# Twelve-layer decoder: the attention stacks written within SBUF instead of by way of DRAM

## The reference

```python
Q = jnp.einsum('bsd,ed->bse', x_q, Wq) + bq
K = jnp.einsum('bsd,ed->bse', x_k, Wk) + bk
Qh, Kh = Q.reshape(b, sq, H, DH), K.reshape(b, -1, H, DH)          # H = 16, DH = 8
scores = jnp.einsum('bqhd,bkhd->bhqk', Qh, Kh) / math.sqrt(DH)
scores = scores + jnp.where(mask[:, None, None, :], 0.0, -1000000000.0)
out = jnp.einsum('bhqk,bkhd->bqhd', jax.nn.softmax(scores), Vh)
```

## Time and profile before

| | us |
|---|---|
| median of 3 runs | 4762.9 (4759.52 to 4770.97) |
| the profiled execution | 4766.7 |
| its span, first to last instruction | 4764.2 |
| TensorE busy | 3496.6 (73%) |
| VectorE busy | 2955.6 (62%) |
| ScalarE, GpSimd busy | 1970.0 (41%), 1234.1 (26%) |
| TensorE's granted clock, mean | 0.833 |

### The profile page before, as it was taken

One profiled execution on the slowest core, in us unless ns is written; L12 is line 12 of the kernel. 1 busy time (PEld: TensorE's weight loads), 2 busy tenths in 40 slices (PEclk: granted clock), 3 DMA queues, 4 the chain that ended last, 5 costly groups with the idle time before them and its releaser, 6 DMA issues. The chain is left out here.

```text
span 4764.2 us, 69288 instructions
## 1 busy us (share of the span) xinstructions
PE 3496.6 (73%) x25546; PEld 2337.3 (49%) x25546; DVE 2955.6 (62%) x6919; ACT 1970.0 (41%) x3470; POOL 1234.1 (26%) x1568
## 2 busy tenths in 40 slices
PE   5868867666878878665886887856589698685674
PEld 3645635334665555433575654533357465352353
DVE  4436874884554785577545488477654548738646
ACT  2423545343343444543344355434235335443333
POOL 0001451550000243253000045145100005516410
PEclk7989978777988988777898998877789799786776
DMA  7110121313121021032122112122211200211321
GB/s 237 46 47 14 39 81 42 103 55 106 66 79 62 28 76 58 29 130 73 47 100 69 39 36 81 45 88 84 104 56 52 98 10 28 80 54 45 117 101 49
DMA packets 174905, 328.00 MB, mean 69 GB/s; under 512 B 13260, under 2 KB 114988, under 8 KB 173740
## 3 DMA queue, kind: packets, MB, share of 16 engines
q1 hardware_dynamic: 174572, 323.59, 20.1%
HBM read 231.87 MB, written 91.67 MB: 68 GB/s over the span
## 5 line engine op out<-in xcount | busy, mean ns | idle before, releaser
L1881 PE MATMUL bank<-sb_big,sb_weights_const 128*128 128x512 f32 x512 | 376.6, 826 | 333.9 <-DVE sb_big L2119 333.2
L1434 POOL TENSOR_TENSOR sb_rs<-sb_ve,sb_weights_const 128x4 f32<-128x4 f32 x112 | 113.4, 1012 | 1757.6 <-DVE sb_ve L1420 1757.3
L1997 POOL TENSOR_TENSOR sb_big<-sb_big 128x512 f32<-128x512 f32 x384 | 496.4, 1307 | 244.9 <-DVE sb_big L2097 244.3
L1958 ACT ACTIVATE bank<-sb_big,sb_Aneg 128x512 f32<-128x512 f32 x512 | 351.7, 689 | 497.4 <-DVE sb_big L2114 392.3
L1252 DVE TENSOR_REDUCE sb_small<-bank 128x4 f32<-128x308 f32 (+1 forms) x512 | 265.9, 523 | 344.5 <-PE bank L967 340.9
L2114 DVE TENSOR_TENSOR_SCAN sb_big<-bank,sb_big 128x512 f32<-128x512 f32 x384 | 464.6, 1210 | 6.6 <-ACT bank L1958 6.3
L988 PE MATMUL bank<-sb_big 128*77 128x128 bf16 (+1 forms) x2560 | 358.1, 234 | 83.7 <-DMA sb_big<-key_parts 30.3
L988 PEld LDWEIGHTS bank<-sb_big 128*77 128x77 bf16 (+1 forms) x2560 | 274.2, 117 | 140.2 <-issue 89.8
L967 PE MATMUL bank<-sb_big 128*128 128x77 bf16 (+1 forms) x2048 | 187.4, 227 | 179.5 <-DMA sb_big<-query_parts 114.2
L1677 PEld LDWEIGHTS bank<-sb_weights_L1f,sb_big 128*128 128x128 f32 x2048 | 257.3, 191 | 109.0 <-issue 104.9
L1137 ACT ACTIVATE sb_big<-bank 77x512 f32<-77x512 f32 (+1 forms) x352 | 207.9, 593 | 228.3 <-PE bank L1009 152.4
(11 more groups left out here) (344 smaller groups left out, 8111.7 us busy)
## 6 DMA issues: line engine op xcount, KB each, us to landing
sb_big<-query_parts SPq DMA_DIRECT2D x160, 512.0 KB, 6.5
sb_big<-state_rows SPq DMA_DIRECT2D x128, 512.0 KB, 3.8
query_parts<-sb_big SPq DMA_DIRECT2D x120, 384.0 KB, 3.3
sb_big<-key_parts SPq DMA_DIRECT2D x64, 512.0 KB, 8.9
sb_big<-context_key_parts SPq DMA_DIRECT2D x64, 308.0 KB, 3.6
key_parts<-sb_big SPq DMA_DIRECT2D x48, 384.0 KB, 4.1
context_key_parts<-sb_big SPq DMA_DIRECT2D x48, 231.0 KB, 4.1
sb_big<-masked_key_parts SPq DMA_DIRECT2D x32, 308.0 KB, 3.5
```

The source lines that it names most:

```text
L1881: pe.matmul(m.bank[s][2][:, :], m.const["ident"], M.h(s, 2 * (n % 2)), start=n == 0, stop=n == NS - 1)\
L1958: act.activation(M.dA(s, half), M.dl(s, half), ACT.Exp, scale=m.Aneg[:, NS * half + n:NS * half + n + 1])\
L1997: pool.tensor_tensor(M.h(s, 2 * (n % 2) + half), M.b_rows(s, n // 2)[:, n % 2, :], M.du(s, half), ALU.mult)\
```

## The change

The stacks are no longer written to DRAM and read back. `heads_stack_sp` takes the place of both helpers: once the low part is made it issues nine transfers from SBUF to SBUF, one for each pair (i, j), each moving one part (128 partitions x 1 KB, for a context's keys 616 bytes) to eight partitions of the stack (16 heads x 1 KB each), and then one that reads the 56 rows below from DRAM, where they still lie since the start. For L1x it first waits for the masked keys' row in DRAM. TensorE waits once, before the first unit, for all ten transfers of both stacks; its waits at the later groups of heads are gone. `heads_sp` no longer has a due time of its own for the reads.

```diff
-    wq="query parts are in DRAM", wk="key parts are in DRAM", wm="the masked keys' row is in DRAM",
-    rq0="query stacks, heads 0 to 3", rq1="query stacks, heads 4 to 7",
...
+    wm="the masked keys' row is in DRAM",
+    rq="a copy of a query part is in its stack", rk="a copy of a key part is in its stack",
...
     def stacks(u):
-        if u % 4 == 0:
-            pe.wait_ge(*g.landed("rq%d" % (u // 4), A.key))
-            pe.wait_ge(*g.landed("rk%d" % (u // 4), A.key))
+        if u == 0:
+            pe.wait_ge(*g.landed("rq", (A.key, "below")))
+            pe.wait_ge(*g.landed("rk", (A.key, "below")))
...
-def heads_write_sp(sp, g, m, A, name):
-    s = g.s
+def heads_stack_sp(sp, g, m, A, name):
+    s = g.s
+    stack = A.q(s) if name == "q" else A.k(s)
     sp.wait_ge(*g.at("proj_d", (A.key, name, "low")))
-    dst = A.dram(s, name)[0:USED].rearrange("(i j d) h n -> (d h) i j n", i=3, j=3)
-    for copy in range(3):
-        sp.dma_start(dst[:, :, copy, :] if name == "q" else dst[:, copy, :, :], A.parts(s, name))\
-          .then_inc(*g.landing("w" + name, (A.key, copy)))
-def heads_read_sp(sp, g, m, A, name):
-    s = g.s
-    for each in name:
-        sp.wait_ge(*g.landed("w" + each, (A.key, 2)))
-    for group in range(4):
-        h = slice(4 * group, 4 * group + 4)
-        for each in name:
-            stack = A.q(s) if each == "q" else A.k(s)
-            sp.dma_start(stack[0:A.rows, h, :], A.dram(s, each)[0:A.rows, h, :])\
-              .then_inc(*g.landing(f"r{each}{group}", A.key))
+    if name == "k" and A.masked:
+        sp.wait_ge(*g.landed("wm", A.key))
+    for i in range(3):
+        for j in range(3):
+            sp.dma_start(stack[8 * (3 * i + j):8 * (3 * i + j) + DH, :, :],
+                         A.parts(s, name)[:, i if name == "q" else j, :])\
+              .then_inc(*g.landing("r" + name, (A.key, i, j)))
+    sp.dma_start(stack[USED:A.rows, :, :], A.dram(s, name)[USED:A.rows, :, :])\
+      .then_inc(*g.landing("r" + name, (A.key, "below")))
...
         yield A.time(A.split_at(i) + 1.1)
-        heads_write_sp(sp, g, m, A, name)
-    yield A.time(A.split_at(len(names) - 1) + 3.5)
-    heads_read_sp(sp, g, m, A, "".join(names))
+        heads_stack_sp(sp, g, m, A, name)
```

More of the change, by code:

```diff
@@ L227 @@
     rb1="an odd pair of rows of B is on all partitions",
-    wq="query parts are in DRAM", wk="key parts are in DRAM", wm="the masked keys' row is in DRAM",
-    rq0="query stacks, heads 0 to 3", rq1="query stacks, heads 4 to 7",
-    rq2="query stacks, heads 8 to 11", rq3="query stacks, heads 12 to 15",
-    rk0="key stacks, heads 0 to 3", rk1="key stacks, heads 4 to 7",
-    rk2="key stacks, heads 8 to 11", rk3="key stacks, heads 12 to 15",
+    wm="the masked keys' row is in DRAM",
+    rq="a copy of a query part is in its stack", rk="a copy of a key part is in its stack",
 )
@@ L1381, in heads_early_sp @@
         yield 0.01
[L1382 to L1386, removed]
+        heads_stack_sp(sp, g, m, A, "k")
 def heads_sp(sp, g, m, A):
```

## The result

The changed kernel takes 5522.1 us (median of 4 runs, 5513.5 to 5531.7) where the kernel before took 4761.2 us on the same chip: a ratio of 1.160, 95% interval 1.1575 to 1.1622. It is slower, as forecast, but by 761 us instead of 451, and 182 us above the upper end of the range.

The account below looks back on a forecast made before the run. Bound: TensorE idle for the stacks, 4% of the span, latency of a way with two legs. Added waits of 539 us x 0.8 = 431, plus 20 for the clock, +451 on 4766.7: 5214 us, range 4760 to 5340.

Parts of the forecast that it names:

- The landing rate, 1.7 us a transfer: Each SBUF-to-SBUF transfer of 128 KB into eight partitions of a stack takes 1.7 us, nine 15.3 us; chance 0.48.
- The upper bound of 5.1 us: Landing in eight partitions at no more than 25.9 GB/s: 5.1 us for 128 KB; as a rival 6480 us, chance 0.04.
- The rows below, 2.5 us,: The tenth transfer of a stack, 0.9 MB from DRAM at 14/16 of 414 GB/s, adds 2.5 us after the nine.
- Issuing: SyncE issues a stack's ten transfers at 0.43 to 0.49 us each, 4.6 us, hidden behind their landing.
- full rate: Rival: a transfer into a stack lands in 0.39 us, SyncE's issuing at 0.43 is the limit; 4712 us, chance 0.13.
- The pass-through of 0.8: Of the 539 us of added wait for stacks, 0.8 reaches the end of the kernel: 431 us.
- single: Context attentions, only the queries' stack waited for: 19.2 us against 8.9, 21 times, 188 us after spare time.
- pair: L0a and L3a, both stacks on the way: 37.0 us against 15.0, 12 times, 259 us after spare time.
- triple: Stream 0's L0a stacks and stream 1's L2x queries together: 54.8 us against 27.6, 3 times, 82 us.
- The clock,: After a wait TensorE goes on at half clock, some 2.5 us lost, newly at about eight waits: 20 us.
- SyncE's queue: The other stream's state rows in L2a queue behind a stack's transfers and come later; counted in the range.
- Only engines are halved: Rival: transfers into a stack use eight engines without crowding, 0.79 us each; 4847 us, chance 0.30.

Follow-up runs that it names:

- e1: Changed kernel with each copy placed on every ninth row of the stack instead of eight neighbouring rows: 4962 us, ratio 1.0428.
- e5: Kernel before, with TensorE waiting ahead of the first unit for all four groups' reads of both stacks: 4920 us, ratio 1.0333.
- e2: Changed kernel with copies on every second row, the ninth copy still on eight neighbouring rows: 5179 us, ratio 1.0903.
- e9: Changed kernel with every ninth row, queries' high and mid copies issued as made, most rows below read during the layer norm: 4787 us, ratio 1.0062.

## Why the prediction was wrong, point by point

- **What bounds the kernel** was right: the added wait reached the end, and the other engines' work did not change.
- **The landing rate, 1.7 us a transfer, is the term that failed most.** Measured 2.0 to 2.2 us (65 to 59 GB/s): the nine were there after some 21 us, where 1.4 + 9 x 1.7 = 16.7 was taken, and the wait grew by 765 us instead of 539. I had worked out 2.1 us from the slow fill and then taken 1.7, on the ground that engines which finish early go on to the next block of partitions. The copies landed one behind the other at an even pace instead. The fill at 376 GB/s, which I weighed against a limit by ports, *reads* 56 rows of SBUF; it said nothing of landing in them. Nor was it typical: the next fills ran at 239 GB/s with the engines as full:

```profile
58.00:62.00 4.00, 1.61 (x15) 1.52 (x14) 2.72 (x16) 0.94 (x2) 1.01 (x1) 0.89 0.96 239
```

A rule of the Trainium skill spoke against the change with an estimated 2.4 us, and I gave it no chance of its own. Put into my sum with the 0.8 kept it gives some 5500, an estimate near the 5522; part of that would have been luck, since 2.4 is too much and 0.8 too little. The upper bound of 5.1 us was never near.
- **The rows below, 2.5 us,** were right as they stood (2 to 3 us behind the nine). With fast copies they are not: in e1 the nine landed after 10 us and the ten after 14.
- **Issuing** was taken as 0.43 to 0.49 us and took 0.61 to 0.65 for a copy; hidden behind the landing, as the prediction said. In the rival "full rate" it would have been the bound, at 5.9 us for nine instead of 3.9.
- **The pass-through of 0.8 is the second failure.** 765 us more waiting made 763 us more span: 1.0. In other runs the waits for the stacks and the span grew as follows: e5 195 and 171 us, e1 204 and 202, e2 378 and 402, so 0.9 to 1.1. The window that suggested less holds the other stream's scan beside a wait of 1.86 us. In a wait of 16.90 us the scan soon stands still, as 662 to 674 shows: its next steps are in the same lists behind steps that need the scores. With 1.0 my own 539 would have given +559, 5326, inside the range; with the measured waits and 0.8 it would have been 5399, outside. Neither alone gives the 5522.
- **The sum, with the measured sizes** (single 24.5, pair 45.8, triple 66.4, in L1x of stream 0 another 5 us a time): 21 x 15.6 - 28 = 300; 12 x 30.8 - 5 = 365; 3 x 38.8 = 116; 4 x 5 = 20: 801, 5% over the 763 of the spans. The patterns and their counts held; two sizes were off.
- **The range** was also summed too low: for 2.1 us a transfer the prediction's own terms give some 5375, where it says 5340 (and some 5090 for 1.4 us, where it says 5080). The measured time is outside either way.
- **The clock,** put at 20 us: the mean fell to 0.788, but TensorE's busy time grew by 17.9 us only, near that term.
- **SyncE's queue** did hold up the state rows, as the prediction feared, though their median stayed at 3.8 us. GpSimd waited for them, and they landed (min/median/max), before:

```profile
  POOL sb_big L1997: 0.5, 2
...
DMA to landing us min/median/max: 3.2/3.8/10.9
```

and after:

```profile
  POOL sb_big L1981: 86.7, 8
...
DMA to landing us min/median/max: 3.2/3.8/20.7
```

TensorE's idle time before the scan's largest line (L1881 before, L1865 now) rose by 6 us only, from 333.9 to 340.1, so nothing says that it reached the end by itself; no run tests it.
- **The signs named beforehand:** 50 to 90 GB/s while a stack lands (59 to 65 seen), landings 1.5 to 2.5 us apart (2.0 to 2.2), issues stretched by a full queue (8.45 to 19.97 us for nine in the triple), the clock under 0.83 (0.788) all came. The ten landings within 17 to 19 us (23.9) and waits of 550 to 750 us (953.7) did not, and that is the landing rate again.
- **The rivals.** "Only engines are halved" (0.79 us, 4847) is near what every ninth row does: 0.8 us a copy, 159 GB/s. It gave 4962; a single took 14 us where the rival had 11.0: the nine were there after 10 and not 8.5, the rows below 4 us later and not 2.5. "Full rate" was reached by no placement: copies alone stayed under 200 GB/s (178 in e9, 1092 to 1098), where 0.39 us a transfer would be 332.

## What to carry to other kernels

A transfer that lands in a few rows of SBUF is priced by which partitions those rows are, not by its bytes or by how busy the DMA engines look: spread its rows so that no two are in one block of four or in blocks 32 apart, and price it from a row that *lands* in SBUF that way. A long way whose legs use all engines can beat a short one that uses half; look first for what of the long way can start earlier, here the writes of the parts that are already made. Where two streams share engines that take their steps in a fixed order, take an added wait at its full length.

## What the runs showed of the hardware that I had not expected

- 128 KB from SBUF into eight partitions: 65 GB/s into eight neighbours, 115 with every second row, 114 with every eighth, 159 with every ninth, at a DMA share of 0.51 to 0.58 throughout; 128 KB at a time from the same partitions into DRAM ran at 270, at the pace of the issues.
- The same score matmuls over 73 rows in place of 128 had a lower granted clock, 0.812 against 0.833 over the whole (0.80 against 0.89 in the stretch of 200 us that differed most), and the kernel was 1.2% slower; with 80 rows, read and multiplied, it was 0.818 and 0.65%. Zero rows that look like waste were worth their place here.
- While TensorE waited 16.90 us for a stack of one stream, no engine did anything for the other stream either from 662 to 674 us: with every engine's steps in a fixed order, one engine's long wait was everyone's.
